# A later step for the reciprocals of the second halves' sums, in a fused attention and expert kernel

## The chip, the cores and the metric

One core of a Trainium2 chip. The metric is device time in microseconds for one execution of the whole kernel, as the median of several runs. A core has five engines that work side by side, each through its own list in order: TensorE (PE in the profile), VectorE (DVE), ScalarE (ACT), GpSimd (POOL) and SyncE (SP), which here issues most of the DMAs. They wait for each other by semaphores.

## What is computed

Attention with a low-rank projection for 4 sequences of 1024 tokens, 16 heads of 16, and behind it a layer of 8 experts in which each token goes to one:

```python
latent = x @ Wc_down                                  # x: normalised (4, 1024, 256)
q = (latent @ Wq_up).reshape(Bsz, Tlen, N_HEAD, HEAD_DIM)
kv = latent @ Wkv_up
k, v = (kv[..., :HEAD_DIM], kv[..., HEAD_DIM:])
att = jnp.einsum('bthd,bsd->bhts', q, k) * scale      # one k and v for all heads
att = jnp.where(causal[None, None], att, -jnp.inf)
att = jax.nn.softmax(att, axis=-1)
y = jnp.einsum('bhts,bsd->bthd', att, v).reshape(Bsz, Tlen, C)
x = x + _layernorm(y @ Wc_proj)
assign = jnp.argmax(logits, axis=-1)                  # logits = x @ centroids.T
h = jax.nn.relu(jnp.einsum('etd,edf->etf', xn, W1) + b1[:, None, :])
y = jnp.einsum('etf,efd->etd', h, W2) + b2[:, None, :]
```

The change touches only the division by the sums of the softmax.

## The kernel before

**Groups and steps.** Attention runs over 16 groups n (4 sequences times 4 groups of 4 heads). A group has 12 steps s. Steps 0 to 3 are the first half (queries 0 to 511, c = 0), steps 4 to 11 the second (queries 512 to 1023, c = 1), each step with one block of 128 keys. In a step TensorE computes scores (L978), ScalarE takes their exponentials (L1066), GpSimd masks the diagonal blocks of steps 0 to 3 and 8 to 11 (L1248), and TensorE multiplies by the values (L995) some steps later. The value matrix has columns of ones, so the same product also gives the sum of each row.

**Events.** Between the scores TensorE works on "events" for the next group: 36 times the raw scores of which VectorE takes row maxima (L947 on TensorE; L1119 or, on the diagonal, L1116 on VectorE), two transposes of finished maxima (L937, L1100), and pieces of the next sequence's projections (L291). A piece costs VectorE two operations, a cast (L1081) and, behind the next event, a residual (L1088). Pieces fall in step 6 of groups 2, 4, 6, 8 and 10 and in some earlier steps of others. Each event fills one of four PSUM banks, the ring; event k may start only once VectorE is done with event k - 4 (`ring_done`). The residual counts as the end of its piece.

**What happens to a half once it is done.** ScalarE copies the 32-row blocks out of PSUM (`out_copy`, L1052): step 6 for the first half, step 2 of the next group for the second. SyncE sends the values to Y and the rows of sums to RC[c] (`send_out`, L1292 and L1294), in step 7, and in step 3 of the next group. Every second group both neighbours' sums are complete in RC[c]; then the pair of groups is finished by four actions in a row, each waiting for the one before:

- VectorE: reciprocal of RC[c] in place (`inverse`, L1130)
- SyncE: store of RC[c] to DRAM (`store_den`, L1299)
- SyncE: load from DRAM spread over the 128 partitions into DEN[c] (`spread_den`, L1304)
- GpSimd: product of Y with DEN[c] (`normalise`, L1228)

For the second halves this is in the even group after the pair: groups 2, 4, ... 14 for seven of the eight pairs. The last pair is finished behind the attention, and the change does not touch it.

**What sets the order.** The order on each engine is written out by step, and nothing is reordered. In a step VectorE first does the step's events and then the reciprocal; SyncE first sends finished maxima (L1284), then `send_out`, then `store_den` and `spread_den`; GpSimd first does the step's mask, then the small operations on finished maxima (L1217 to L1221), then the product. Behind attention stand the routing (L731 to L914) and the experts (L1429 on).

Of the kernel before, what the change touches and what calls it, by code (L numbers as in the profile page):

```python
# [48 lines left out]
LAST = len(STEPS) - 1  # L49
# [51 lines left out]
def piece_no(b, name):  # L101
    return (b - 1) * len(ORDER) + ORDER.index(name)
# [134 lines left out]
def attention(nc, eps, eps2, spare, xv, Wc_down, Wq_up, Wkv_up, Wc_proj, centroids, ident, identb, Y, W1s, w1_v, w1_in,  # L237
# [3 lines left out]
    with ExitStack() as ctx:  # L241
# [836 lines left out]
        def _(dve):  # L1078
# [49 lines left out]
            def inverse(n, c):  # L1128
                dve.wait_ge(o_out[c], 32 * (n + 1))
                dve.reciprocal(RC[c][:, :], RC[c][:, :]).then_inc(inverted, 1)  # L1130
# [37 lines left out]
            for n in range(NB):  # L1168
                for s in range(len(STEPS)):
                    events(EVENT_AT[NU * n + UNIT_AT[s]], EVENT_AT[NU * n + UNIT_AT[s + 1]])  # L1170
                    if n == NB - 1 and s == 4:
                        centre_rows()
                    if n == NB - 1 and s == 7:
                        dve.wait_ge(wp_turned, 1)
                        dve.tensor_copy(R1[:, :], ring[0]).then_inc(wp_step, 1)
                    if n == NB - 1 and s == 8:
                        dve.wait_ge(wp_turned, 2)
                        dve.tensor_copy(Wpx[:, :, D:D + E], ring[1][:, 0:DC * E].rearrange("p (c e) -> p c e", c=DC))\
                            .then_inc(wp_step, 1)
                    if s == C0 + 6 and n % 2:  # L1180
                        inverse(n, 0)
                    if s == 5 and n and n % 2 == 0:
                        inverse(n - 1, 1)
            route_vector(dve, 0, 1)
            inverse(NB - 1, 1)
# [3 lines left out]
        @block.gpsimd  # L1189
        def _(pool):  # L1190
            def third(b, name, left):
                pool.wait_ge(part2, piece_no(b, name) + 1)
                parts_sent(pool, b, name)
                _, p2, p3 = parts(name)
                pool.tensor_tensor(p3, left, p2, ALU.subtract).then_inc(part3, 1)

            def split_max(r, c):

                k = EVENTS.index(("max", r, SET_LAST[c]))
                pool.wait_ge(ring_done, DONE_AT[k])  # L1200
                if r:
                    pool.wait_ge(ring_ready, EVENTS.index(("m", r - 1, c)) + 1)
                if c:
                    pool.wait_ge(merged, r + 1)
                alone(pool, spare)
                base = M_STEPS * (QC * r + c)
                step = [0]

                def then(op):

                    step[0] += 1
                    op.then_inc(m_step, 1)
                    pool.wait_ge(m_step, base + step[0])

                n0, n1, n2 = (NMX[c][:, a, :] for a in range(3))
                top = mx[:, :] if c else MP[r % 2][:, 0, :]
                then(pool.tensor_scalar(n0, top, -1.0, None, ALU.mult))  # L1217
                then(pool.tensor_tensor(mr[:, 0, :], top, n0, ALU.add))
                then(pool.tensor_scalar(n1, mr[:, 0, :], -1.0, None, ALU.mult))
                then(pool.tensor_tensor(mr[:, 1, :], mr[:, 0, :], n1, ALU.add))  # L1220
                pool.tensor_scalar(n2, mr[:, 1, :], -1.0, None, ALU.mult).then_inc(nmx_ready, 1)  # L1221

            def normalise(n, c):

                b, g = divmod(n, NG)
                pool.wait_ge(den_in[c], 16 * (n // 2 + 1))
                y = YT[:, g // 2, b * T + c * NQ:b * T + (c + 1) * NQ]
                pool.tensor_tensor(y, y, DEN[c], ALU.mult).then_inc(normed, 1)  # L1228

            def splits(lo, hi):  # L1230

                for k in range(lo, hi):
                    kind, r, n = EVENTS[k]
                    if kind == "max" and n in SET_LAST:
                        split_max(r, SET_LAST.index(n))

            norm_gpsimd(pool)
            splits(0, EVENT_AT[0])
            for n in range(NB):
                b, g = divmod(n, NG)  # L1240
                for s in range(len(STEPS)):
                    t = len(STEPS) * n + s
                    if s in DIAG:
                        off = STEPS[s][2]
                        pool.wait_ge(exp_done, NU * n + UNIT_AT[s + 1])
                        alone(pool, spare)
                        p = PR[t % RB][:, :, off:off + P]
                        pool.affine_select(out=p, in_=p, compare_op=ALU.is_ge, fill=0.0, base=0,  # L1248
                                           pattern=[[0, GH], [1, P]], channel_multiplier=-1).then_inc(masked, 1)
                    splits(EVENT_AT[NU * n + UNIT_AT[s]], EVENT_AT[NU * n + UNIT_AT[s + 1]])  # L1250
                    for name in PIECES:
                        if (g, s - 2) == PIECES[name] and b < B - 1:
                            third(b + 1, name, R1[0:rows_of(name), :])
                    if s == 1 and n and n % 2 == 0:
                        normalise(n - 1, 0)
                    if s == 10 and n and n % 2 == 0:
                        normalise(n - 1, 1)
            normalise(NB - 1, 0)
            route_masks(pool)
            normalise(NB - 1, 1)  # L1260
            for k in range(RX):
                pool.wait_ge(x1_out[k], 16 * (NQD // RX))
            pool.wait_ge(idx_ready, 1)
            gather_first(pool, Y, x1_rows, IDX, first_x, 0)

        @block.sync
        def _(sp):
# [48 lines left out]
            for n in range(NB):  # L1316
                b, g = divmod(n, NG)
                for s in range(len(STEPS)):
                    if n == 0 and s in (5, 9):
                        queries(0, 2 if s == 5 else 3)  # L1320
                    if s == 4 and n == 2:
                        sp.wait_ge(lt_copied, N1)
                        sp.wait_ge(first3, len(FIRST))
                        sp.wait_ge(lx_done, B)
                    if s == 4 and n == NB - 3:
                        sp.dma_start(Wpx[:, :, 0:D], Wc_proj.rearrange("(c p) n -> p c n", p=P)).then_inc(wp_in, 16)
                        for last in (("piece", B - 1, "q11"), ("values", B - 1, None)):
                            sp.wait_ge(ring_ready, EVENTS.index(last) + 1)
                        for g in range(NG):
                            sp.wait_ge(q_in[g], 16 * QC * len(QPART) * B)  # L1330
                        load_w2(sp, W2s, w2_v, w2_in, E - 1)
                        for k in range(RX):
                            sp.dma_start(rows_in(LT, k), xv[:, k * QT:(k + 1) * QT, :]).then_inc(xr_in[k], 16)
                    if s == 4 and n >= NB - 2:
                        sp.wait_ge(exp_done, NU * n)
                        for e in ((0, 1), (2,))[n - NB + 2]:
                            load_w2(sp, W2s, w2_v, w2_in, e)
                    if s == 4 and n < LATE:
                        sp.dma_start(W1s[:, :, n * F:(n + 1) * F], w1_v[n]).then_inc(w1_in, 16)
                    if b < B - 1:  # L1340
                        if s == 1 and g:
                            sp.wait_ge(exp_done, NU * n)
                            queries(b + 1, g - 1)
                        if (g, s) == KEYS_AT:
                            keys(b + 1)
                    if s == 1 and g == 0 and b:
                        sp.wait_ge(exp_done, NU * n)
                        queries(b, NG - 1)
                    sends(EVENT_AT[NU * n + UNIT_AT[s]], EVENT_AT[NU * n + UNIT_AT[s + 1]])
                    if s == 3 and n:  # L1350
                        send_out(n - 1, 1)
                    if s == C0 + 4:
                        send_out(n, 0)
                    if n % 2 and s == C0 + 7:
                        store_den(n, 0)
                    if n % 2 and s == C0 + 8:
                        spread_den(n, 0)
                    if n and n % 2 == 0 and s == 6:
                        store_den(n - 1, 1)
                    if n and n % 2 == 0 and s == 8:  # L1360
                        spread_den(n - 1, 1)
            send_out(NB - 1, 1)
            sp.wait_ge(st_ready, NU * NB)
# [323 lines left out]
```

## Time and profile before

| | |
|---|---|
| runs shown | 893.13 us median of 3 (892.67 to 896.02) |
| the profiled execution | 891.93 us |
| its span, first to last instruction | 890.2 us |
| mean granted TensorE clock | 0.961 of full speed |
| PE busy | 829.3 us (93%) |
| DVE busy | 638.1 us (72%) |
| ACT busy | 551.6 us (62%) |
| POOL busy | 288.9 us (32%) |

Times in the rows are microseconds from the start of the span; a line number is that of the kernel. In a timeline row the two numbers are start and duration; brackets behind it hold the idle time of the engine before the row and what ended it. The page's busy time of PE counts overlapping matmuls once. Operations of VectorE can overlap a little in the records, so the distance from one start to the next is the safer measure of what one costs.

### The profile page before, as it was taken

To read this page: it belongs to the slowest core of one execution; us is meant where nothing else is said; L and a number is where in the kernel's file an instruction comes from. 1 tells how busy PE (TensorE), PEld (TensorE's weight loads), DVE (VectorE), ACT (ScalarE), POOL (GpSimd) and SP (SyncE) were. 2 spreads that over 40 slices of the span, in tenths; PEclk is the share of its full clock that TensorE was granted. 3 is DMA by queue.
4 is the path that set the end of the run, shared out by engine and by line. 5 is a ranking of instruction groups with operands and counts; after the bars stand their busy time and mean duration, and the time that the engine had idled before them with its cause. 6 is when DMAs were issued, how large, how long until landed. Compare 5 with 4: busy or idle time off the path is not lost. (4 is left out here: it accounts for less than half of the span.)

```text
span 890.2 us, 20228 instructions
## 1 busy us (share of the span) xinstructions
PE 829.3 (93%) x5520; PEld 495.5 (56%) x5521; DVE 638.1 (72%) x2133; ACT 551.6 (62%) x1244; POOL 288.9 (32%) x547
## 2 busy tenths in 40 slices
PE   7999999999999999999999999549999999999993
PEld 3533333333433334333333338349999999999993
DVE  7789889898888898879889606835555555555552
ACT  3624767776767777667767776145666666666661
POOL 4502322442244233432233222042433333344211
PEclk8977999999999999999999999669999999999998
DMA  6111233222311111101233227930011100110000
GB/s 202 41 41 61 82 102 111 67 69 86 104 59 47 39 59 53 55 28 51 75 114 105 84 79 245 332 98 19 29 34 33 35 29 26 35 31 20 20 22 1
DMA packets 55764, 62.92 MB, mean 71 GB/s; under 512 B 13166, under 2 KB 47366, under 8 KB 55568
## 3 DMA queue, kind: packets, MB, share of 16 engines
q1 hardware_dynamic: 51952, 53.71, 18.5%
q0 software_dynamic: 3744, 8.40, 3.1%
q8 instruction: 31, 0.51, 0.3%
q14 instruction: 37, 0.30, 0.1%
HBM read 36.12 MB, written 9.57 MB: 51 GB/s over the span
## 5 line engine op out<-in xcount | busy, mean ns | idle before, releaser
L1066 ACT ACTIVATE W2s<-bank 128x512 f32<-128x512 f32 (+1 forms) x512 | 257.2, 572 | 127.5 <-PE bank L978 125.2
L1116 DVE CUSTOM_DVE_ANT_0 room_kv<-bank,causal 128x384 bf16<-128x384 f32 (+3 forms) x512 | 220.9, 486 | 32.3 <-PE bank L947 31.0
L978 PE MATMUL bank<-W2s,room_kv 99*128 99x512 bf16 (+3 forms) x768 | 226.5, 332 | 4.6 <-ACT W1s L1066 2.8
L947 PE MATMUL bank<-room_kv,W2s 96*128 96x512 bf16 (+3 forms) x768 | 223.6, 337 | 7.5 <-DVE R L1088 5.5
L1119 DVE TENSOR_REDUCE MP<-bank 128x1 f32<-128x512 f32 x256 | 162.5, 680 | 14.8 <-PE bank L947 14.7
L1248 POOL TENSOR_SCALAR_AFFINE_SELECT W2s<-W2s 128x512 f32<-128x512 f32 x96 | 61.2, 637 | 297.0 <-ACT W2s L1066 294.9
L1520 PE MATMUL hp<-XNT,LT 128*128 128x128 f32 x1248 | 148.4, 278 | 2.5 <-DVE XNT L1596 2.5
L1520 PEld LDWEIGHTS hp<-XNT,LT 128*128 128x128 f32 x1248 | 147.8, 195 | 5.1 <-DVE XNT L1596 3.1
L978 PEld LDWEIGHTS bank<-W2s,room_kv 99*128 99x128 bf16 x768 | 68.3, 98 | 145.2 <-ACT W2s L1066 63.8
L1528 PE MATMUL yp<-W2s,LT 128*128 x624 | 141.2, 379 | 0.7 <-DVE z L1608 0.7
L995 PE MATMUL bank<-W2s,room_kv 128*32 128x512 f32 (+2 forms) x1152 | 129.0, 532 | 0.2 <-ACT W1s L1052 0.2
L1528 PEld LDWEIGHTS yp<-W2s,LT 128*128 128x128 f32 x624 | 115.5, 190 | 15.2 <-issue 1.1
L947 PEld LDWEIGHTS bank<-room_kv,W2s 96*128 96x128 bf16 x768 | 74.9, 99 | 75.1 <-DVE MP L1119 11.1
L1560 ACT ACTIVATE LT<-W1s 128x1024 f32 x78 | 78.4, 1050 | 39.0 <-PEq L241 22.2
L1478 POOL DMA_INDIRECT out_dram<-O,io x39 | 39.7, 1018 | 141.0 <-DVE O L1653 141.0
L1570 ACT ACTIVATE LT<-hp,PT 128x128 f32<-128x128 f32 x312 | 84.2, 378 | 0.4 <-issue 0.4
L1550 ACT ACTIVATE sdf<-mvf,eps 128x2 f32<-128x2 f32 (+1 forms) x43 | 12.7, 296 | 99.0 <-DVE mvf L1631 99.0
L1066 ACT ACTIVATE W1s<-bank 128x512 f32<-128x512 f32 x96 | 53.8, 630 | 18.2 <-PE bank L978 18.1
L1596 DVE TENSOR_SCALAR XNT<-xp,PT 128x128 f32<-128x128 f32 x78 | 28.5, 406 | 39.7 <-PE xp L1508 39.7
L995 PEld LDWEIGHTS bank<-W2s,room_kv 128*32 128x32 f32 x1152 | 26.8, 108 | 49.0 <-issue 28.7
L1608 DVE TENSOR_TENSOR z<-yp,b2s 128x256 f32<-128x256 f32 x39 | 16.6, 425 | 42.3 <-PE yp L1528 42.3
L1116 DVE DVE_READ_ACCUMULATOR2_ANT MP<- 128x1 f32 x512 | 42.3, 83 | 0.0
(185 smaller groups left out, 774.3 us busy)
## 6 DMA issues: line engine op xcount, KB each, us to landing
W2s<-W2s SPq DMA_DIRECT2D x160, 64.0 KB, 2.6
W1s<-in_L_ffn_W_dram SPq DMA_DIRECT2D x8, 1024.0 KB, 5.5
W2s<-in_L_ffn_W_dram SPq DMA_DIRECT2D x8, 1024.0 KB, 7.5
Y<-in_L_attn_x_dram SPq DMA_DIRECT2D x8, 512.0 KB, 7.4
Y<-W1s SPq DMA_DIRECT2D x32, 128.0 KB
W1s<-den_rows SPq DMA_DIRECT2D x16, 256.0 KB
LT<-in_L_attn_x_dram SPq DMA_DIRECT2D x8, 512.0 KB, 6.6
x_rows<-LT SPq DMA_DIRECT2D x8, 512.0 KB, 4.1
```

The source lines that it names most:

```text
L947: last = pe.matmul(bank[:, at:at + w], Q[0:NR, g, i // BW, h, i % BW * P:(i % BW + 1) * P], K[b % 2][0:NR, k * NQ:k * NQ + w], start=True, ...
L978: last = pe.matmul(dst[:, i, :], K[b % 2][0:KR, j * P:(j + 1) * P], Q[0:KR, g, c, h, off:NQ], start=True, stop=True)
L995: last = pe.matmul(OB[32 * h:32 * h + 32, off:NQ], V[n // NG % 2][:, j, :, :].rearrange("p d u -> p (d u)"), PR[(len(STEPS) * n + s) % RB] ...
L1066: act.activation(PR[t % RB][:, heads[0]:heads[-1] + 1, off:NQ], unit_of(ST[(NU * n + u) % STB], s), ACT.Exp, scale=SCALE).then_inc(exp_don ...
L1116: op = dve.tensor_tensor_reduce(junk[:, done % 2, at:at + w], src, causal[:, NQ - w:NQ], 1.0, LOWEST, ALU.add, ALU.max, dst)
L1119: op = dve.tensor_reduce(dst, src, AX, ALU.max)
L1248: pool.affine_select(out=p, in_=p, compare_op=ALU.is_ge, fill=0.0, base=0, pattern=[[0, GH], [1, P]], channel_multiplier=-1).then_inc(mask ...
L1478: pool.indirect_dma_start(out=out.rearrange("b t d -> (b t) d"), out_offset=bass.IndirectOffsetOnAxis(ap=io[:, :], axis=0), in_=O[:, :], i ...
L1520: mm = pe.matmul(hp[k][i][:, f, :], WS[:, c, at:at + P], XNT[:, c, :], start=c == 0, stop=c == DC - 1)
L1528: mm = pe.matmul(yp[:, :], HT[k][:, f, :], W2s[:, ds(e, 1), f * D:(f + 1) * D], start=f == 0, stop=f == FC - 1)
L1560: act.activation(WS[:, :, i * NQ:(i + 1) * NQ], W1s[:, :, ds(e * F + i * NQ, NQ)], ACT.Copy)\
L1570: act.activation(HT[k][:, ff, :], hp[k][i][:, f, :], ACT.Relu, bias=PT[:, 2 * DC + ff, ds(e, 1)]).then_inc(relued, 1)
```

## The change

In even groups from 2 on, four actions on the second half of the group before are moved: the reciprocal from step 5 to step 7, its store from 6 to 8, the spread from 8 to 9, and GpSimd's product from step 10 to step 11. In every case they stay behind the step's other work on that engine. The first halves, and the last pair, keep their places. No instruction is added or removed.

```diff
                     if s == C0 + 6 and n % 2:
                         inverse(n, 0)
-                    if s == 5 and n and n % 2 == 0:
+                    if s == 7 and n and n % 2 == 0:
                         inverse(n - 1, 1)
...
                     if s == 1 and n and n % 2 == 0:
                         normalise(n - 1, 0)
-                    if s == 10 and n and n % 2 == 0:
+                    if s == LAST and n and n % 2 == 0:
                         normalise(n - 1, 1)
...
                     if n % 2 and s == C0 + 8:
                         spread_den(n, 0)
-                    if n and n % 2 == 0 and s == 6:
+                    if n and n % 2 == 0 and s == 8:
                         store_den(n - 1, 1)
-                    if n and n % 2 == 0 and s == 8:
+                    if n and n % 2 == 0 and s == 9:
                         spread_den(n - 1, 1)
```

## Rows read from the trace of the kernel before

**Rows 1.** The page, part 1: busy time, share, matmuls.

```profile
PE 829.3 (93%) x5520; PEld 495.5 (56%) x5521; DVE 638.1 (72%) x2133; ACT 551.6 (62%) x1244; POOL 288.9 (32%) x547
```

**Rows 2.** All waits: engine line, waited for: total us, times, longest.

```profile
POOL Y L1228 <- DMA W1s<-den_rows: 6.0, 1, 6.0
PE bank L947 <- DVE R L1088: 5.5, 7, 1.2
...
DVE RC L1130 <- DMA RC<-W1s: 3.0, 4, 1.1
```

**Rows 3.** Timeline of DVE, step 6 of group 2: start, us, operation, idle before.

```profile
147.41 0.35 DVE L1130 RECIPROCAL RC<-RC 128x32 f32<-128x32 f32 x1 [0.62 <-DMA RC<-W1s]
...
148.22 0.68 DVE L1081 CAST W2s<-bank 128x512 bf16<-128x512 f32 x1
...
149.41 0.68 DVE L1088 TENSOR_TENSOR R<-bank,W2s 128x512 f32<-128x512 f32 x1
```

**Rows 4.** Timeline of DVE, the same cast in groups 4, 6 and 10.

```profile
205.60 0.67 DVE L1081 CAST W2s<-bank 128x512 bf16<-128x512 f32 x1
...
264.74 0.67 DVE L1081 CAST W2s<-bank 128x512 bf16<-128x512 f32 x1
...
381.24 0.67 DVE L1081 CAST W2s<-bank 128x512 bf16<-128x512 f32 x1
```

**Rows 5.** Timeline of PE, the piece's two matmuls in groups 2, 4, 6, 10.

```profile
146.30 1.02 PE L291 MATMUL bank<-LT,WqT 128*128 128x512 f32 x2
...
203.31 1.02 PE L291 MATMUL bank<-LT,WqT 128*128 128x512 f32 x2
...
263.46 1.02 PE L291 MATMUL bank<-LT,WqT 128*128 128x512 f32 x2
...
378.87 1.02 PE L291 MATMUL bank<-LT,WqT 128*128 128x512 f32 x2
```

**Rows 6.** Timeline of PE, its waits for VectorE in groups 2, 4 and 10.

```profile
150.15 0.39 PE L947 MATMUL bank<-room_kv,W2s 96*128 96x512 bf16 x1 [1.18 <-DVE R L1088]
...
207.53 0.39 PE L947 MATMUL bank<-room_kv,W2s 96*128 96x512 bf16 x1 [1.18 <-DVE R L1088]
...
381.38 0.39 PE L947 MATMUL bank<-room_kv,W2s 96*128 96x512 bf16 x1 [0.40 <-DVE MP L1119]
...
383.17 0.39 PE L947 MATMUL bank<-room_kv,W2s 96*128 96x512 bf16 x1 [1.18 <-DVE R L1088]
```

**Rows 7.** Timeline of PE, last maxima of steps 6 and 7, groups 3 and 12.

```profile
176.50 0.38 PE L947 MATMUL bank<-room_kv,W2s 96*128 96x512 bf16 x1
...
178.71 0.38 PE L947 MATMUL bank<-room_kv,W2s 96*128 96x512 bf16 x1
...
439.04 0.38 PE L947 MATMUL bank<-room_kv,W2s 96*128 96x512 bf16 x1
...
441.47 0.39 PE L947 MATMUL bank<-room_kv,W2s 96*128 96x512 bf16 x1
```

**Rows 8.** Group 10: window, length, busy PE PEld DVE ACT POOL, granted clock, DMA share, GB/s.

```profile
383.50:386.90 3.40, 3.40 (x15) 0.81 (x12) 3.27 (x7) 2.31 (x4) 0.00 (x0) 0.50 0.32 112
386.90:391.00 4.10, 4.10 (x32) 1.53 (x25) 2.82 (x12) 2.43 (x5) 0.93 (x2) 1.00 0.00 0
```

**Rows 9.** Timelines of SP, POOL and PE: spread, product, first values of group 3.

```profile
151.86 0.63 SPq L1304 DMA_DIRECT2D W1s<-den_rows  x1
...
162.17 1.27 POOL L1228 TENSOR_TENSOR Y<-Y,W1s 128x512 f32<-128x512 f32 x1
...
168.11 1.07 PE L995 MATMUL bank<-W2s,room_kv 128*32 128x512 f32 x8
```

**Rows 10.** Busy time by window as in rows 8, step 9 of group 2.

```profile
155.50:157.00 1.50, 1.50 (x14) 0.81 (x10) 1.50 (x11) 1.00 (x3) 1.50 (x2) 1.00 0.00 0
```

**Rows 11.** Timelines of DVE and PE, step 9 of group 2: bank freed, bank refilled.

```profile
155.50 0.08 DVE L1116 DVE_READ_ACCUMULATOR2_ANT MP<- 128x1 f32 x1
...
156.57 0.38 PE L947 MATMUL bank<-room_kv,W2s 96*128 96x256 bf16 x2
```

## Prediction, made from the rows above

> **What bounds the kernel now.** I read the page first. TensorE (PE) is busy 93% of the span [rows 1], and in the attention part it hardly ever stands still. So a change inside attention can only win what PE loses there to other engines. The list of waits says who holds PE up [rows 2]. The largest line in this part is the maximum pass (L947) waiting for VectorE's residual (L1088): 5.5 us in 7 waits. The same list has VectorE's reciprocal (L1130) waiting for the DMA that brings the sums, 3.0 us in 4 waits. The question is whether the two are the same loss.
>
> The timeline of group 2 says yes. VectorE is free at 146.79 (147.41 less 0.62 of idle), but the reciprocal of group 1's second half stands next in its order and its sums have not landed. It starts at 147.41; the cast of the projected piece follows at 148.22 and the residual at 149.41, ending at 150.09 [rows 3]. That residual frees the ring bank which PE wants next: PE's matmul starts at 150.15, after 1.18 us of waiting [rows 6]. VectorE is a queue with no slack just there, because step 6 of groups 2, 4, 6, 8 and 10 carries an extra piece (cast and residual) beside its four maxima. So whatever stands in VectorE's way ahead of step 6 reaches PE in full.
>
> **What is moved, part by part.** Seven reciprocals (groups 2, 4, ... 14) go from behind step 5's events to behind step 7's.
>
> First, step 6. Without the reciprocal and its wait VectorE goes on at once, but not without limit: the cast needs the piece's two matmuls. These end at 147.32 in group 2 (146.30 + 1.02), 204.33 in group 4, 264.48 in group 6 and 379.89 in group 10 [rows 5]. Allowing 0.05 us for the signal, the cast can start at 147.37, 204.38, 264.53 and 379.94. It starts today at 148.22, 205.60, 264.74 and 381.24 [rows 3, 4]. So the chain cast, maximum, residual moves up by:
> - group 2: 148.22 - 147.37 = 0.85 us
> - group 4: 205.60 - 204.38 = 1.22
> - group 6: 264.74 - 264.53 = 0.21
> - group 8 repeats group 6's pattern (no wait for the DMA, the reciprocal alone): 0.2
> - group 10: 381.24 - 379.94 = 1.30
>
> Does PE follow? Its waits are 1.18 us in groups 2 and 10 [rows 6] with a shorter one (0.40) just ahead in group 10, so PE can take all of these; it keeps a rest of 0.3 us or less, set by the piece itself. In groups 12 and 14 no piece comes. Step 7's four maxima there run from the last maximum of step 6 to their own last: 439.04 to 441.47, 2.43 us, in group 12, against 176.50 to 178.71, 2.21 us, in group 3, which has no reciprocal there [rows 7]. Gain 0.22 in group 12; in group 14 I take 0. Sum: 0.85 + 1.22 + 0.21 + 0.2 + 1.30 + 0.22 = 4.0 us. Bounds: 0 (PE finds another releaser at once) and 5.5 + 0.4 = 5.9 (every wait on that line goes, with the shorter one).
>
> Second, the clock. The granted clock is 0.50 (1.2 GHz) in the 3.4 us from 383.5 on, and 1.00 (2.4 GHz) in the stretch behind it [rows 8]. The fall follows directly on group 10's two waits, 1.6 us of idle together [rows 6], the largest sum in attention. With 1.3 us of that gone I expect no fall. PE is busy throughout the stretch (3.40 of 3.40), so half clock costs half of it, 1.7 us. Bounds: 1.7 if it goes, 0 if it stays or only changes place, -1.7 if the new order brings a second one.
>
> Third, what step 7 has to carry now: one reciprocal a group, 0.35 us at most [rows 3]. VectorE has no idle time after it (busy 1.50 of 1.50 us in step 9, [rows 10]), so the cost isn't hidden there; it is hidden in the ring's depth. PE waits for a maximum only four events later. In step 9 of group 2 the bank that is freed at 155.58 is written from 156.57 on [rows 11]: 0.99 us to spare, and 0.35 uses up a third of it. The wait for sums is gone as well, since they landed by 147.41 and the reciprocal now comes near 153. Cost 0; if the cover were gone it would be 7 x 0.35 = 2.5 us; a gain is excluded, since the same work is only done later.
>
> Fourth, SyncE's queue. The store of the reciprocals moves from step 6 to 8 and the spread from step 8 to 9. The store no longer stands ahead of group n's own output DMAs of step 7, which wait for ScalarE's copy anyway: 0. The spread is issued at 151.86 [rows 9]; the DMAs are at rest from 155.5 on [rows 10], so it takes at most 3.6 us to land. From the reciprocal's start to the spread's issue there are 4.5 us today (147.41 to 151.86), an upper bound for what the store needs between them. In the changed kernel: reciprocal near 153, spread issued by 157.5, landed by 161.1, and probably two to three us sooner. Behind it on SyncE nothing is due before the next group. Cost 0.
>
> Fifth, GpSimd's product. Today it starts at 162.17 and takes 1.27 us [rows 9], and the group's last mask comes behind it. Now it comes behind that mask, so near 162 again, with group 2 running 0.9 us earlier; the spread has landed by 161.1 at the latest. Cost 0; and 0 gain, since in these rows PE doesn't wait for this mask.
>
> A rule speaks against this part. The Trainium skill, page "DMA: Bandwidth & Descriptors", section "Rules for kernel authors", says to issue a DMA early and to wait for it late. The change does the opposite: the issue moves by two steps and the consumer by one. The rows of the last paragraph show the cover that is left, so by them the rule costs nothing here; its result otherwise is the slow rival below.
>
> **Sum.** The profiled execution took 891.93 us (span 890.2 and 1.7 around it), 1.2 us under the median of 893.13. 4.0 + 1.7 = 5.7 us less: 886.2 for that execution, 887.4 for the median. Nothing after attention is tied to a fixed time: routing and experts start from attention's end, so the gain should arrive whole.
>
> **Rivals.**
> (a) *The clock stretch stays.* For: groups 2 and 4 have the same wait of 1.18 us [rows 6] and no fall, so it doesn't force one, and what does may come from the phase of an execution. Against: it begins within 0.4 us of the largest wait. Gain 4.0 alone: 893.13 - 4.0 = 889.1. The Trainium skill, page "TensorE: Matmul & The Clock Gate", says under "HAM oscillation" that waits much longer than these bring the clock down, and under "A second HAM failure mode" that short idles between groups of matmuls can do it too. By the first the stretch isn't the waits' work, by the second it is; no row here decides, and both times are given above.
> (b) *Step 7 becomes the new place of the queue.* PE's maxima of steps 8 and 9 wait for the shifted reciprocal in full. For: VectorE has no idle time there. Against: the 0.99 us. 4.0 - 2.5 = 1.5 us gained: 891.6.
> (c) *The change gives nothing*, because ScalarE or another bank takes over as PE's releaser at once. For: ScalarE's exponentials feed PE in the same steps. Against: in group 3, with no reciprocal and no piece, PE goes through step 7 in 2.21 us [rows 7], so they let it pass. 893.1.
> (d) *Slower, by GpSimd.* The spread lands too late, GpSimd stands at the product, and behind it the next group's masks wait, then PE's value matmuls. The last product waited 6.0 us for its spread [rows 2]. If each of the seven did, the product would end near 162.2 + 6.0 + 1.3 = 169.5 and the next group's first mask later still, while PE wants that mask at 168.11 [rows 9], less the 0.9 us that it is ahead: 2.3 us lost a group, 7 x 2.3 = 16, less 4: 905. It decides from a landing near 165 on, 8 us after the issue, against the 3.6 seen.
>
> **How the numbers follow.** Chances: forecast 0.53, (a) 0.31, (b) 0.07, (c) 0.04, (d) 0.05. Predicted 887.4. About 0.5% (4.5 us, a time of 888.7) is what a measurement of this kernel can tell from no change. Around each case I allow 1.5 us, since the three runs before span 3.4 us: the forecast clears 888.7 in about 0.85 of its chance, (a) in 0.3 of its. Faster 0.45 + 0.10 = 0.55, slower 0.05, and 0.40 within. The range runs from 884.9 (the upper bound of 5.9 and the clock's 1.7, with some scatter) to 891.2 (past (a), most of the way to (b)).
>
> **What would show it.** In the profile after: the reciprocal's waits for the sums (3.0 us) gone; PE's waits on L1088 in groups 2, 4 and 10 down from 1.18 to near 0.3 us and their total from 5.5 to about 2; no stretch at 0.50 between 80 and 560 us; group 10 shorter by 3 us, groups 2 and 4 by about 1; no new wait on L947 in steps 8 and 9; L1228 without a wait but its last. The prediction is wrong if PE's waits turn up under another name in step 7, or if the low clock only changes place.

## The result, and the profile after

The changed kernel takes **886.01 us** (median of 10 runs, 884.95 to 890.21). The kernel before takes 893.43 (10 runs, 891.52 to 898.48) on the same chip. The ratio is 0.992, interval 0.9901 to 0.9938: faster by 0.8%. The forecast was 887.4, range 884.9 to 891.2. The profiled execution took 886.19 us (span 884.5) against 891.93 (span 890.2): 5.7 us less, the sum that was forecast for it.

The page after, part 1, and one group of part 5 (busy, mean ns of one, idle before and what ended most of it):

```profile
PE 826.5 (93%) x5520; PEld 495.6 (56%) x5521; DVE 638.1 (72%) x2133; ACT 550.5 (62%) x1244; POOL 287.8 (33%) x547
...
L947 PE MATMUL bank<-room_kv,W2s 96*128 96x512 bf16 (+3 forms) x768 | 222.7, 336 | 4.4 <-DVE R L1088 2.7
```

Against [rows 1] PE is 2.8 us less busy with the same 5520 matmuls, and no other engine's work changes by more than 1.1 us. Fewer busy microseconds for the same matmuls: up to 1.7 are the stretch at half clock, below. The rest, 1.1, are probably short gaps, which this figure counts as busy, since a matmul's 0.38 us reach past the next one's start 0.22 later. The rest of the gain, 2.9 us, is plain idle time. The list of waits after:

```profile
PE bank L947 <- DVE R L1088: 2.7, 6, 0.5
...
POOL Y L1228 <- DMA W1s<-den_rows: 6.4, 1, 6.4
```

In [rows 2] the first line was 5.5 us in 7 waits, 1.2 the longest. VectorE's line L1130, 3.0 us, is in the list no more. GpSimd's product (L1228) waits once, as before: for the last group's spread.

VectorE in step 6 and 7 of group 2, after (start, us, operation):

```profile
146.96 0.69 DVE L1119 TENSOR_REDUCE MP<-bank 128x1 f32<-128x512 f32 x1
147.61 0.69 DVE L1081 CAST W2s<-bank 128x512 bf16<-128x512 f32 x1
148.22 0.68 DVE L1119 TENSOR_REDUCE MP<-bank 128x1 f32<-128x512 f32 x1
148.82 0.68 DVE L1088 TENSOR_TENSOR R<-bank,W2s 128x512 f32<-128x512 f32 x1
...
153.01 0.34 DVE L1130 RECIPROCAL RC<-RC 128x32 f32<-128x32 f32 x1
153.28 0.63 DVE L1119 TENSOR_REDUCE MP<-bank 128x1 f32<-128x512 f32 x1
```

The maximum now starts at 146.96, the moment VectorE is free, where [rows 3] shows 0.62 us of idle and then the reciprocal. The reciprocal stands in step 7, at 153.01, without a wait. PE in the same place after, in its timeline (idle before and releaser in brackets):

```profile
146.55 1.02 PE L291 MATMUL bank<-LT,WqT 128*128 128x512 f32 x2
...
148.50 0.38 PE L947 MATMUL bank<-room_kv,W2s 96*128 96x512 bf16 x1
...
149.56 0.39 PE L947 MATMUL bank<-room_kv,W2s 96*128 96x512 bf16 x1 [0.45 <-DVE R L1088]
```

The wait is 0.45 us where [rows 6] has 1.18. The piece ends at 147.57 (146.55 + 1.02) and the cast starts 0.04 later. So the piece, not VectorE's queue, is what comes late now.

The granted clock around group 10 (window, length, busy PE PEld DVE ACT POOL, clock, DMA share, GB/s), after:

```profile
379.00:383.00 4.00, 3.55 (x20) 1.12 (x20) 4.00 (x8) 3.75 (x9) 0.00 (x0) 1.00 0.10 35
383.00:387.00 4.00, 4.00 (x30) 1.62 (x32) 4.00 (x20) 3.27 (x8) 1.75 (x2) 1.00 0.10 25
```

The clock is at its upper level, 2.4 GHz, throughout. In [rows 8] it was at 1.2 GHz for 3.4 us here.

**The gain by group.** This table is worked out from the traces: the distance from a group's first score matmul (L978) to the next group's, in us. "Attention" runs from group 1's start to the last value matmul. The groups left out are the same within 0.1 in before and after.

| kernel | 2 | 4 | 6 | 8 | 10 | 12 | attention |
|---|---|---|---|---|---|---|---|
| before | 29.7 | 30.1 | 29.1 | 29.0 | 31.8 | 28.1 | 429.0 |
| after | 28.9 | 28.9 | 28.9 | 28.9 | 28.9 | 27.9 | 423.3 |
| gain | 0.8 | 1.2 | 0.2 | 0.1 | 2.9 | 0.2 | 5.7 |
| forecast | 0.85 | 1.22 | 0.21 | 0.2 | 1.30 + 1.7 | 0.22 | 5.7 |

The routing behind it takes 58.3 us in both. The experts take 300.4 us, then 300.1, and group 1 starts 0.3 us later in after (102.7 against 102.4); neither is the change's work, and the two cancel. So the gain arrives whole.

### The profile page after: what moved, and what is told of

It reads as the page before. It is cut to its first block and busy times, and to the rows that moved or that the text cites. A ratio compares the mean times of both kernels' runs of the same rounds, so it can differ in the third digit from the quotient of the medians.

```text
span 884.5 us, 20228 instructions
## 1 busy us (share of the span) xinstructions
PE 826.5 (93%) x5520; PEld 495.6 (56%) x5521; DVE 638.1 (72%) x2133; ACT 550.5 (62%) x1244; POOL 287.8 (33%) x547
## 5 line engine op out<-in xcount | busy, mean ns | idle before, releaser
L1116 DVE CUSTOM_DVE_ANT_0 room_kv<-bank,causal 128x384 bf16<-128x384 f32 (+3 forms) x512 | 220.5, 485 | 31.7 <-PE bank L947 30.4
L978 PE MATMUL bank<-W2s,room_kv 99*128 99x512 bf16 (+3 forms) x768 | 225.9, 331 | 5.1 <-ACT W1s L1066 3.3
L978 PEld LDWEIGHTS bank<-W2s,room_kv 99*128 99x128 bf16 x768 | 68.3, 98 | 146.5 <-ACT W2s L1066 64.6
L1596 DVE TENSOR_SCALAR XNT<-xp,PT 128x128 f32<-128x128 f32 x78 | 28.4, 406 | 39.2 <-PE xp L1508 39.2
L1618 DVE BATCH_NORM_STATS2 stf<-Y 128x6 f32 (+1 forms) x39 | 16.6, 427 | 35.2 <-issue 28.8
```

The source lines that it names most:

```text
L978: last = pe.matmul(dst[:, i, :], K[b % 2][0:KR, j * P:(j + 1) * P], Q[0:KR, g, c, h, off:NQ], start=True, stop=True)
L1116: op = dve.tensor_tensor_reduce(junk[:, done % 2, at:at + w], src, causal[:, NQ - w:NQ], 1.0, LOWEST, ALU.add, ALU.max, dst)
```

## The experiments

The theory has two terms: PE loses 4.0 us because VectorE comes late to step 6, and 1.7 us because the clock falls behind the longest of these waits. What was open: is it the reciprocal or its queues, the wait or the work, does the clock follow from the waits, and is the new place free. Each ratio is to the kernel before on the same chip, with its interval.

**1. The kernel before once more.** No edit.

> The kernel before, once more, to see each run's mean granted clock. The medians differ by 7.4 us (893.4 against 886.0), the two profiled spans by 5.7. Theory A (the clock falls in more places than the profiled execution shows): the runs that take longer have a lower mean clock, about 0.001 of it for each 0.9 us, since a stretch of 1.8 us at half clock lowers the mean of an 890 us span by 0.001 and costs 0.9 us; the fastest runs have 0.961 to 0.963, those above 895 us 0.957 or less. Theory B (the rest is something else, DMA landing times for instance): no such order between clock and time. Time 893.4, within 1 us, ratio 1.000.

Measured 891.96 us, ratio 1.0018 [0.9994, 1.0041]. The groups have the lengths of the first trace within 0.1 us, but for group 4 (29.8, not 30.1), and the clock falls at 383.2, again for 3.4 us. So both the groups' lengths and this fall repeat. The time of one execution is less steady, 889.8 to 900.0, and follows the mean clock: over the 36 runs of this kernel in this comparison the median is 895.6 us at a mean clock of 0.955 (3 runs) and 890.3 at 0.962 (6 runs). Above 0.962 the order ends: the four runs at 0.965 and 0.966 have a median of 891.3.

**2. Only the reciprocal.** Before, with VectorE's line alone:

```diff
-                    if s == 5 and n and n % 2 == 0:
+                    if s == 7 and n and n % 2 == 0:
                         inverse(n - 1, 1)
```

> Only VectorE's reciprocal goes from step 5 to step 7; store, spread and product keep their steps (6, 8, 10). Theory A (all of the gain is VectorE's way ahead of the piece in step 6): 886.0, a ratio of 0.992 as with the whole change; PE's waits for L1088 are 0.45 us in groups 2 to 10. Rival (the queues' moves matter): the store in step 6 now holds SyncE up for some 5 us and with it the next DMAs of step 7, and the product of step 10 may wait; then 888 to 893.

Measured 886.56 us, ratio 0.9943 [0.9922, 0.9964]. PE's waits are 0.45 us in groups 2 to 10, and every group but the last, group 15, is as long as in after. This one line carries the waits term whole. SyncE paid a little for it, in its timeline:

```profile
152.65 0.36 SPq L1299 DMA_DIRECT2D den_rows<-RC  x1
153.06 0.52 SPq L1292 DMA_DIRECT2D Y<-W1s  x1
```

The store, still in step 6's place, waits for the later reciprocal and holds group 2's own output DMA until 153.06, against 149.92 in after. Nobody waits for that DMA at this point. The clock fell in this trace too, but at 515.1, in group 15, where the kernel before shows no fall; group 15 takes 27.9 us here, 25.1 in after.

**3. Only the queues.** After, with the reciprocal back in step 5: the other three hunks alone.

> Only store, spread and product move (to steps 8, 9 and 11); the reciprocal stays in step 5. Theory A: no change, 893.4, ratio between 0.999 and 1.001; the waits of 1.18 us for L1088 and the reciprocal's 3 us for its DMA are as in the kernel before. Rival (the queues' moves give part of the gain, by fewer DMAs at once in steps 6 to 8 or a mask that comes sooner): 888 to 892.

Measured 892.25 us, ratio 1.0015 [0.9998, 1.0033]: nothing. PE's five waits are there (1.10, 1.18, 0.64, 0.60, and 0.60 with 1.18 in group 10), and so is L1130's wait for the DMA (2.6 us). But behind them the clock held:

```profile
382.00:386.00 4.00, 3.99 (x23) 1.45 (x24) 4.00 (x8) 3.02 (x6) 0.00 (x0) 1.00 0.23 77
```

Two things follow. The store, the spread and the product are worth nothing by themselves. And a wait doesn't force a fall. This trace shows the waits without the clock's part: attention takes 426.9 us, 3.6 more than after. That is the waits term measured alone, against a forecast of 4.0, with waits that differ a little from those of before (group 4 takes 29.7 us here and 30.1 there). Group 10 takes 30.4 us here, with waits 0.2 us longer than before's, and 31.8 in before. So the fall cost before some 1.4 to 1.6 us, and not the 1.7 of the forecast.

**4. The wait away, the reciprocal left in step 5.** Before, with the row sums' DMA sent ahead of the output's and on a semaphore of its own:

```diff
+                past(sp, den_out[c], 16 * (n // 2))
+                sp.dma_start(RC[c][rows, :], OS[c][1:P:2 * HD, :]).then_inc(sums_in[c], 16)
                 sp.dma_start(y, OS[c][0:P:2, :]).then_inc(o_out[c], 16)
...
-                dve.wait_ge(o_out[c], 32 * (n + 1))
+                dve.wait_ge(sums_in[c], 16 * (n + 1))
```

> The kernel before, but the row sums are sent ahead of the values and have a semaphore of their own, so that the reciprocal in step 5 no longer waits for the values' DMA (issued 0.6 us ahead of it). The reciprocal itself stays in step 5. By the rows of before the four waits of 0.62, 0.99, 1.07 and 0.30 us (3.0) should lose 0.6 us or more each, so about 2 us of them goes and 0.7 to 1 stays; the reciprocal's own 0.27 us in each group stays. Theory A (the wait is most of the loss): PE's waits in groups 2, 4 and 10 fall from 1.18 to 0.7 or 0.9 us, gain some 2 us by the waits and up to 2 more if the clock no longer falls: 889 to 891.5. Rival (only the reciprocal's position counts): 893.4.

Measured 886.75 us, ratio 0.9943 [0.9923, 0.9962], below the band that was expected: a miss. VectorE, step 6 of group 2:

```profile
146.90 0.35 DVE L1132 RECIPROCAL RC<-RC 128x32 f32<-128x32 f32 x1
147.16 0.63 DVE L1121 TENSOR_REDUCE MP<-bank 128x1 f32<-128x512 f32 x1
147.71 0.68 DVE L1083 CAST W2s<-bank 128x512 bf16<-128x512 f32 x1
```

The reciprocal is in its old place but waits no more, and the cast starts at 147.71, within 0.1 us of after's 147.61. PE:

```profile
149.63 0.39 PE L948 MATMUL bank<-room_kv,W2s 96*128 96x512 bf16 x1 [0.59 <-DVE R L1090]
```

0.59 us against 0.45, groups of 29.0 or 29.1 against 28.9. So the reciprocal's own work costs 0.14 us a group here (29.01 against 28.87), and 0.2 in groups 6 and 8 of before, where it waits for no DMA. In groups 2, 4 and 10 the wait for the DMA was most of the loss. I had put too much on the work. Group 12 takes 27.6 us here, 0.3 less than in after: PE's wait for GpSimd (L938 here, L937 in after) is 0.62 us, not 0.91. Why GpSimd comes sooner wasn't looked into.

**5. The changed kernel again, and its seven reciprocals taken out.** In the second of these each moved reciprocal is a bare increment of its semaphore, so the second halves of seven groups are not divided by their sums.

> The changed kernel once more, beside its variants on one chip. Theory A: 4.0 us of PE's waits less in every run, seen best in the fastest runs of both kernels (889.4 before, 885.4 after, 0.5 around it); and a clock that falls in fewer runs, so that the medians differ by 4.5 to 6. Vector alone gave 0.9943 of before; this should give the same, 0.993 to 0.995. Rival (the whole change gains more than VectorE's part, as the first comparison's 0.992 suggests): 0.990 to 0.992.

> The changed kernel with the seven moved reciprocals left out (a bare semaphore increment in their place in step 7), so the second halves are multiplied by their sums and not divided. Asks what a reciprocal in step 7 still costs. Theory A (0: the ring's depth hides it, 0.90 us to spare in step 9 with it in place): the same time as the changed kernel within 0.5 us, ratio to it 1.000. Rival (b), the new place costs 7 x 0.27 to 0.35 = 1.9 to 2.5 us: 2 us faster than the changed kernel.

Measured 886.92 us, 0.9939 [0.9914, 0.9965], and 886.31 us, 0.9924 [0.9894, 0.9953]. The groups are 28.9 us in both. The reciprocal in step 7 costs nothing that can be seen.

**6. How deep is the cover of step 7?** After, with six more reciprocals ahead of the moved one:

```diff
+                if c and n < NB - 1:
+                    for i in range(6):
+                        dve.reciprocal(load[:, i, :], RC[c][:, :])
                 dve.reciprocal(RC[c][:, :], RC[c][:, :]).then_inc(inverted, 1)
```

> The changed kernel with six further reciprocals of the same shape, into a tile that nobody reads, ahead of each of the seven in step 7: 6 x 0.27 = 1.6 us more for VectorE there. Theory A (the cover is the 0.90 us to spare of step 9 in groups 2 to 10 and 1.15 in groups 12 and 14): PE loses 1.6 - 0.9 = 0.7 us in five groups and 0.45 in two, together 4.4 us, all in steps 8 and 9, in waits for L1116 or L1119: 890.2 where the changed kernel has 885.8. Rival (no cover, all is paid): 11 us, 897. Rival (idle time takes it all): 0.

Measured 889.59 us, 0.996 [0.9938, 0.9982], 2.7 us over after in the same comparison. VectorE, step 7 of group 2:

```profile
152.45 1.40 DVE L1133 RECIPROCAL load<-RC 128x32 f32<-128x32 f32 x6
153.77 0.30 DVE L1134 RECIPROCAL RC<-RC 128x32 f32<-128x32 f32 x1
```

Six take 1.32 us (153.77 - 152.45), 0.22 each, not the 0.27 that I took. The groups grow by 0.50 to 0.56 us in 2 to 10 and by 0.32 in 12 and 14; attention by 3.5. The bank of [rows 11] is freed and refilled in after, without the load, at

```profile
155.11 0.08 DVE L1116 DVE_READ_ACCUMULATOR2_ANT MP<- 128x1 f32 x1
...
155.98 0.38 PE L947 MATMUL bank<-room_kv,W2s 96*128 96x256 bf16 x2
```

Freed at 155.19, refilled from 155.98: 0.79 us, where [rows 11] had 0.99 (the expectation's 0.90 was misread). Where PE does wait it starts 0.06 us behind the freeing (150.09 in [rows 3], 150.15 in [rows 6]), so 0.73 us can be used up. 1.32 - 0.73 = 0.59 us should reach PE in groups 2 to 10. In groups 12 and 14 the same distance is 1.04 us, so 0.34 should. Both fit: the cover is real, it is as deep as it reads, and beyond it the cost comes through one for one. My expected 4.4 was too high because six reciprocals are shorter than I took them.

**7. Does work in step 5 alone bring the loss back?** After, with four needless reciprocals behind step 5. By its condition (`n < NB - 3`, NB is 16) the load stands in groups 2 to 12, six groups; the expectation counts five:

```diff
+                    if s == 5 and n and n % 2 == 0 and n < NB - 3:
+                        for i in range(4):
+                            dve.reciprocal(load[:, i, :], ident[:, 0:32])
```

> The changed kernel with four reciprocals that nobody needs and that wait for nothing, behind step 5's events in groups 2, 4, 6, 8 and 10: 4 x 0.27 = 1.1 us of VectorE time in the place where the reciprocal used to stand. Theory A (whatever stands ahead of the piece in step 6 reaches PE in full): each of the five groups has PE waiting 0.45 + about 1.0 us behind the piece, 5 x 1.0 = 5 us more: 890.8. And if such a wait brings the clock down, the profile shows one or more stretches at 0.50 behind those waits, each 1.7 us more. Rival (the wait for the DMA was the cost, not VectorE's time in step 5): under 2 us.

Measured 890.77 us, 0.9985 [0.9961, 1.0009], 3.9 over after. PE, group 2, and the same in groups 4, 6, 8 and 10:

```profile
149.89 0.39 PE L948 MATMUL bank<-room_kv,W2s 96*128 96x512 bf16 x1 [1.18 <-DVE R L1089]
```

With no DMA wait anywhere, VectorE's lateness makes the very wait of [rows 6], and each of these groups takes 29.65 us, nearly what group 2 took before (29.73). Group 12, which has no piece, takes 28.4 us against 27.9. The clock falls behind none of the six; it falls at 519.2, in group 15, for 10.2 us.

**8. Longer waits, for the clock.** The same, in the same six groups, with ten instead of four.

> As the changed kernel with four needless reciprocals in step 5 of groups 2 to 10, but with ten: 10 x 0.22 = 2.2 us of VectorE time ahead of the piece (the six in step 7 were spaced 0.22 us). Two questions. The price: theory A has PE lose 2.2 us in each of five groups, groups of 31.1 us against 28.9, 11 us in all by the waits alone: 897. The clock: if waits of VectorE's kind bring it down, the profile shows stretches at 0.50 behind several of the five piece waits, each 1.7 us more, and the time goes beyond 900. If the clock falls for another reason (the stretches of some executions at 515 to 519 us, in group 15, had no such wait before them), it stays at 1.00 behind all five.

Measured 906.24 us, 1.0158 [1.0111, 1.0206]. PE waits 1.14 and then 1.18 us in each of groups 2 to 10, and 1.57 us once in group 12. The windows behind the waits of groups 2, 4, 6, 8, 10 and 12:

```profile
150.50:153.90 3.40, 3.40 (x11) 0.97 (x14) 3.24 (x7) 2.00 (x4) 0.00 (x0) 0.51 0.03 5
211.00:214.40 3.40, 3.40 (x22) 1.15 (x20) 3.40 (x8) 3.08 (x7) 0.00 (x0) 1.00 0.00 0
271.00:274.40 3.40, 3.24 (x18) 1.07 (x19) 3.40 (x8) 2.28 (x5) 0.00 (x0) 1.00 0.04 10
330.00:333.40 3.40, 3.40 (x21) 1.20 (x20) 3.40 (x8) 3.08 (x7) 0.00 (x0) 1.00 0.00 0
389.50:396.30 6.80, 6.01 (x18) 1.52 (x19) 4.78 (x10) 2.95 (x6) 0.00 (x0) 0.50 0.08 23
450.90:454.30 3.40, 3.40 (x13) 0.50 (x12) 3.03 (x7) 1.06 (x2) 0.00 (x0) 0.50 0.00 0
```

The clock is halved behind three of them and full behind the other three, although groups 2 to 10 had the same two waits. From group 1 on the clock falls nowhere else in this attention. The timed runs agree: three of the six have a mean clock of 0.950 or less, where the lowest of the 20 runs of after is 0.957, and the slowest (913.2 us) has the lowest clock, 0.945. So short waits bring the clock down, some of the time. Where it fell, the group is longer: 32.5 and 33.7 us for groups 2 and 10 against 30.9 for 4, 6 and 8. Each halved stretch costs a little under half its length: 1.6 for 3.4 us, 2.8 for 6.8.

Three traces now show what VectorE's lateness costs. What stands in step 5 puts its next maximum off by 0.26 us in experiment 4 (146.90 to 147.16), by 0.90 in experiment 7 (146.52 to 147.42) and by 2.17 here (145.77 to 147.94). Group 6, in which the clock held in all three, takes 29.01, 29.65 and 30.92 us against 28.87 in after: 0.14, 0.78 and 2.05 more. Each time 0.12 us is absorbed and the rest reaches PE.

**9. Is step 7 itself needed?** After, with the reciprocal behind step 6 instead (`s == 6`).

> The changed kernel with the reciprocal behind step 6's events in place of step 7's; store, spread and product as in the change. It then stands behind the piece and step 6's maxima, and ahead of step 7's. Theory A (only what stands ahead of the piece counts): PE's waits behind the piece stay 0.45 us, groups 2 to 10 last 28.9 us, attention from group 1 on 423.3; time as the changed kernel, a ratio of 0.993 to 0.995. Rival (each step in which VectorE is behind pays for it): groups of 29.1 or more, attention 424.5 or more.

Measured 887.05 us, 0.9937 [0.9915, 0.9958]; groups 28.9, waits 0.46 us. The same as step 7. It is enough that it stands behind the piece's residual and not ahead of it.

**10. The spread in step 11 instead of 9**, SyncE's line of after alone, to press on the rival that GpSimd comes late.

> The changed kernel with the spread issued in step 11 in place of step 9, some 5.5 us later, so that it is the last thing before the product that needs it. Asks how much cover the product has: by the rows of the changed kernel the spread of group 2 would be issued near 160.5 and land within 3.6 us, by 164; the product would start there and not at 162.16, and end by 165.4, where the next group's first mask starts at 164.39 today and PE wants it at 167.5. Theory A: GpSimd waits up to 2 us in seven places for W1s<-den_rows, some 5 to 13 us in all beside the last one's 6.4, and PE loses nothing: the changed kernel's time, ratio to before 0.993 to 0.995, attention from group 1 on 423.3. Rival (d) in small (GpSimd's waits reach PE through the masks): 0.5 to 2 us a group, 3.5 to 14 us more.

Measured 885.26 us, 0.9932 [0.9917, 0.9946]; GpSimd's product at 161.99 and without a wait. This one tells nothing about that rival. SyncE, in its timeline:

```profile
153.21 0.35 SPq L1299 DMA_DIRECT2D den_rows<-RC  x1
154.65 0.63 SPq L1304 DMA_DIRECT2D W1s<-den_rows  x1
164.25 0.76 SPq L1284 DMA_DIRECT2D W2s<-MT  x1
```

The spread is issued at 154.65 as in after (154.83). SyncE has nothing else to do between steps 9 and 11, so its step number changed nothing in time. The 5.5 us that the expectation counted on didn't come about. How late the spread may land before GpSimd holds PE up wasn't measured.

**11. Can the remaining 0.45 us go as well?** After, with a piece's residual directly behind its cast, and the order in which banks come free written to match:

```diff
-    if EVENTS[event][0] != "piece":
-        DONE.append(event)
-    if event and EVENTS[event - 1][0] == "piece":
-        DONE.append(event - 1)
+    DONE.append(event)
...
-                    if k and EVENTS[k - 1][0] == "piece":
-                        residual(k - 1)
+                    if kind == "piece":
+                        residual(k)
```

> The changed kernel, and the residual of every piece runs directly behind its cast, not behind the next event's maximum; the ring counts it in that order. It aims at the 0.45 us that PE still waits behind the piece. Theory A (the piece's bank is then free 0.6 us sooner and the next one 0.6 later, for which 1.10 us are to spare): PE's wait of 0.45 goes in groups 2, 4, 6, 8 and 10 and in group 0, some 2 to 2.7 us: groups 2 to 10 last 28.5, attention 421 to 421.5, ratio to before 0.990 to 0.992. Rival (the residual now waits for the end of the cast on its own engine, and the next maximum pays): the same 28.9 or more.

Measured 884.57 us, 0.9902 [0.9869, 0.9936], attention 421.7 us, 1.6 less than after. The sum came near what was expected, but not from the groups I had in mind. The 0.45 us waits are gone, yet groups 2 to 10 still take 28.9. PE there:

```profile
148.49 0.39 PE L944 MATMUL bank<-room_kv,W2s 96*128 96x512 bf16 x1
...
149.09 0.39 PE L944 MATMUL bank<-room_kv,W2s 96*128 96x512 bf16 x1
...
149.68 0.39 PE L944 MATMUL bank<-room_kv,W2s 96*128 96x512 bf16 x1
...
150.28 0.39 PE L944 MATMUL bank<-room_kv,W2s 96*128 96x512 bf16 x1
```

They come 0.6 us apart, the pace of VectorE's maxima, where after has 0.44 apart behind one wait. The same loss is spread over four small steps, too small for the list of waits. The gain is in groups 1, 5 and 9, from 30.0 to 29.5 each: there the wait of L937 for L1088 (1.5 us in 3 waits, before and after alike) goes. It is the best version that was run. Its interval overlaps that of after, so the timed runs alone don't separate the two; the trace does.

## Why the prediction was right, point by point

**The bound and the waits term: right, within 0.4 us.** Forecast 4.0 us; measured alone 3.6, by the kernel of experiment 3. In the pair of traces it is what the clock's 1.4 to 1.6 leave of 5.7, so 4.1 to 4.3. Outside group 10 it fits group by group to 0.1, since the term was taken at the right place: the cast starts 0.04 us behind the piece's end, for which 0.05 was allowed. The other limit, PE's remaining wait, was mis-sized: "0.3 us or less", measured 0.45 in five groups. In group 2 the gain of 0.85 still came whole, because PE had lost a further 0.12 us in a gap too short for the list of waits: two maxima stand 0.55 apart (147.81 to 148.36) in before, 0.43 (148.07 to 148.50) in after. That the sum, 5.7, came out to 0.1 is partly luck: the waits term differs between executions by a few tenths, and the clock term was 0.1 to 0.3 too large.

**"The same loss": shown.** Experiment 4 removes only the wait for the DMA and gets nearly all; experiment 7 adds only work, a delay of 0.90 us, and makes groups 2 to 10 nearly as long as group 2 was. VectorE's lateness ahead of step 6 is the cause, whatever makes it late. It doesn't reach PE "in full", as the prediction has it: 0.12 us of it is absorbed (experiments 4, 7 and 8).

**The clock term: right in the profile, a chance in a timed run.** The fall behind group 10 is gone in both traces of after and stands in both of before. But experiment 3 has the waits and no fall, 7 has them and none, and in experiments 2, 7 and 10 the clock fell in group 15, where this change removes nothing. So rival (a) was partly right: the waits don't force a fall. Experiment 8 shows that they can bring one, in 3 of 6 places.

The timed runs point the same way. Of the 92 runs of the kernel before whose mean clock is on record, 52 have 0.961 or less (57%); of the 58 runs of the seven kernels without the long wait (after twice, experiments 2, 4, 9, 10 and the one without reciprocals) it is 12 (21%). The mean clock doesn't count falls in attention, though. Other parts of the kernel run at half clock too, and for lengths that vary: both traces of before, each with one fall, have 0.961, the trace of experiment 2, with a fall, has 0.964, and that of experiment 11, with none behind group 0, has 0.960. With 0.960 as the limit the counts are 27 and 10 (29% and 17%), which says little.

How the time differs: 4.2 us between the fastest runs (888.92, and 884.77 for after), 4.6 between the medians of the runs with a mean clock of 0.962 (890.6 in 16 runs, 886.0 in 8), 5.8 between all medians (892.0, and 886.17 over 20 runs of after). I read the first two as the waits term and the 1.2 to 1.6 more as the clock's, but the two weren't separated in timed runs: experiment 3's kernel, whose trace has no fall, is in the median as slow as before. What decides whether a given wait brings a fall stays open. The Trainium skill, page "TensorE: Matmul & The Clock Gate", names under "A second HAM failure mode" short idles between groups of matmuls as a cause, and under "HAM oscillation" waits far longer than these. The rows of experiment 8 agree with the first: no idle of PE in that attention is longer than 1.57 us.

**Step 7's reciprocal at no cost: shown** (experiment 5), and its cover too: 0.99 us was read in [rows 11], and 0.79 is left, more than the 0.64 that taking 0.35 off would give. Experiment 6 fits a cost that starts there, less 0.06, in both kinds of group. Rival (b) falls. It would need 0.73 us more work in step 7, between three and four more reciprocals.

**SyncE and GpSimd at no cost: held, partly tested.** Experiments 2 and 3 show that these moves neither cost nor bring anything. The store takes 1.4 us to land: issued at 153.39, the spread behind it at 154.83, well within the bound of 4.5. The product starts at 162.16, forecast "near 162". The rule that the prediction cites from the Trainium skill, page "DMA: Bandwidth & Descriptors", section "Rules for kernel authors", has two halves. Issuing the store and the spread later costs nothing here. Waiting late is what the change does for the sums: the reciprocal that waited 0.62 us for them in [rows 3] waits for nothing at 153.01. I had read the rule as only against the change. But experiment 10 didn't move the spread in time, so rival (d) is refuted for this kernel, not measured beyond it.

**Rival (c)**, another releaser at once: falls for the 3.6 us of the waits. It holds for what was tried next. In experiment 11 another limit of the same engine took over in full in groups 2 to 10.

## What to carry to other kernels

When a small operation stands in an in-order engine's queue and waits for a DMA, look at what is queued behind it and at how much slack the consumer has there; here 0.35 us of work with its wait cost 0.9 us in group 2 and 1.2 in group 4. Read the slack of the new place as the time between freeing a buffer and refilling it: here it is 0.79 us, and experiment 6 fits a cost that begins within 0.06 of that. A list of waits leaves out short gaps, so a wait that goes away may come back as a slower pace; compare the lengths of whole stages too.

## What the hardware did that I had not expected

- The clock fell behind PE waits of 1.14 and 1.18 us in groups 2 and 10, and not behind the same waits in groups 4, 6 and 8 of the same execution (experiment 8).
- It fell for 6.8 to 10.2 us in group 15 in experiments 2, 7 and 10, and in neither trace of after, with the same work there. These falls, too, come within 0.8 us of a short idle of PE, here 0.59 us for ScalarE (ended at 514.57, 519.24 and 515.12; the clock fell at 515.1, 519.2 and 515.9). After has the same wait, ended at 515.28, and no fall.
- Reciprocals of 128x32 that read the same tile follow each other after 0.22 us, though a single one lasts 0.34 to 0.35 and the next operation starts 0.27 behind it.
- Ahead of the tightest step VectorE's delays reach PE all but 0.12 us, whether the delay is 0.26, 0.90 or 2.17 us (experiments 4, 7 and 8).
